# Stacked and exact parts in a linear attention's two kinds of products, with SyncE copies between partitions, and three seams reordered

## What is computed

```python
q, k, v = x @ Wq, x @ Wk, x @ Wv                    # 16 heads of 16
gk = log_sigmoid(x @ Wgk1 @ Wgk2 + bgk2) / 16       # decay of each feature
def step(state, inp):
    qt, kt, vt, gt = inp
    state = state * exp(gt)[..., None] + vt[..., None] * kt[..., None, :]
    return state, einsum('bhvk,bhk->bhv', state, qt)
out = layernorm(outs) * gamma + beta
out = (out * silu(x @ Wg)) @ Wout
x = x + out * silu(mixture_of_adapters(x))          # first layer
x = x + window_attention(x) * silu(ternary_mlp(x))  # second layer, left out here
```

## Time and profile before

| | us |
|---|---|
| median of 3 runs (3458.78 to 3458.85) | 3458.81 |
| the profiled execution | 3460.7 |
| its span in the trace | 3459.0 |
| from chunk 0 of one sequence to that of the next | 212.0 |

### The profile page before, as it was taken

How to read it: one execution, slowest core, us unless ns; L and a number is a source line. 1 busy time by engine, 2 the same in 40 slices (tenths; PEclk the granted TensorE clock), 3 DMA queues, 4 the chain that set the end, 5 groups by cost and what they waited for, 6 DMA issues and landing times.

```text
span 3459.0 us, 88576 instructions
## 1 busy us (share of the span) xinstructions
PE 3342.5 (97%) x34556; PEld 2274.0 (66%) x34556; DVE 2607.4 (75%) x6329; ACT 1863.8 (54%) x4135; POOL 1273.4 (37%) x1393
## 2 busy tenths in 40 slices
PE   6999999999999999999999999999999999999998
PEld 3676666766666666666666666666676666766666
DVE  6777867778677777877778777786777867778777
ACT  3364654646546465463655636456364653646546
POOL 4424244242442524325233342423434244242442
PEclk8999999999999999999999999999999999999999
DMA  4001010010110101011010100101001010010110
GB/s 105 18 22 47 24 38 19 24 44 24 38 23 24 40 24 47 14 38 26 24 50 11 50 18 20 49 12 49 18 23 45 24 38 23 20 44 24 38 23 26
DMA packets 98479, 109.59 MB, mean 32 GB/s; under 512 B 21153, under 2 KB 75025, under 8 KB 98065
## 3 DMA queue, kind: packets, MB, share of 16 engines
q1 hardware_dynamic: 93200, 102.25, 11.3%
q10 hardware_dynamic: 4864, 1.69, 0.2%
HBM read 74.01 MB, written 17.30 MB: 26 GB/s over the span
## 4 chain that ended last, share of the span: by engine, by line
PE 75%; DVE 12%; ACT 5%; issue 5%; POOL 1%; DMA 0%; DVEq 0%; SPq 0%; ACTq 0%; POOLq 0%
PE bank L1549 6%; PE bank L1508 5%; PE bank L1879 5%; PE bank L1647 5%; PE bank L1529 5%; PE bank L1781 5%; PE bank L1897 4%; PE bank L1719 4%; PE bank L1664 3%; PE bank L1619 3%; PE bank L1816 3%; PE bank L1842 3%; PE bank L1604 3%; PE bank L1713 2%; DVE am L1245 2%
## 5 line engine op out<-in xcount | busy, mean ns | idle before, releaser
L867 POOL TENSOR_TENSOR qx<-qx 128x512 f32<-128x512 f32 x256 | 277.3, 1088 | 658.7 <-ACT qx L1113 657.8
L1470 DVE TENSOR_TENSOR sq_lo<-qx,sq_hi 128x512 fp32r<-128x512 f32 x256 | 224.1, 875 | 177.1 <-ACT sq_hi L1092 176.6
L1378 DVE TENSOR_REDUCE row_max<-bank 128x4 f32<-128x384 f32 x512 | 270.8, 550 | 95.4 <-PE bank L1781 95.0
L1245 DVE TENSOR_TENSOR am<-bank,causal 128x512 f32<-128x512 f32 x512 | 328.1, 683 | 11.3 <-PE bank L1619 11.3
L988 ACT ACTIVATE tanh_g<-bank 128x256 f32<-128x256 f32 x128 | 49.3, 385 | 394.9 <-PE bank L1508 394.9
L1508 PE MATMUL bank<-w_vg,xt 128*128 128x512 f32 x512 | 252.3, 615 | 0.0
L1549 PE MATMUL bank<-xt,w_down 128*128 128x512 f32 x512 | 237.2, 596 | 0.0
L1897 PE MATMUL bank<-sq_hi,pj_t 128*128 128x512 f32 x512 | 213.2, 416 | 14.8 <-DVE sq_lo L1470 10.3
L1387 DVE TENSOR_TENSOR am<-bank,row_max 128x384 f32<-128x384 f32 x384 | 212.8, 554 | 9.8
L1113 ACT ACTIVATE qx<-bank,scale_fc 128x512 f32<-128x512 f32 x256 | 177.9, 695 | 70.9 <-PE bank L1884 69.0
L1032 ACT ACTIVATE am<-am 128x384 f32<-128x384 f32 x384 | 202.9, 528 | 8.5 <-DVE am L1387 8.5
(11 more groups left out here) (264 smaller groups left out, 8671.4 us busy)
## 6 DMA issues: line engine op xcount, KB each, us to landing
g_wide<-gate_rows SPq DMA_DIRECT2D x64, 512.0 KB, 6.0
x<-in_L_attn_x SPq DMA_DIRECT2D x128, 128.0 KB, 2.3
qt<-in_L_attn_x SPq DMA_DIRECT2D x128, 128.0 KB, 2.6
out<-x SPq DMA_DIRECT2D x128, 128.0 KB, 1.7
k<-k SPq DMA_DIRECT2D x96, 128.0 KB, 2.4
qt<-in_L_attn_x ACTq DMA_DIRECT2D x8, 128.0 KB, 7.6
x<-in_L_ffn_w_fc SPq DMA_DIRECT2D x1, 1024.0 KB, 5.9
attn<-in_L_ffn_w_proj SPq DMA_DIRECT2D x1, 1024.0 KB, 8.7
```

The lines of the kernel that those rows point to most:

```text
L867: nc.gpsimd.tensor_tensor(sq[:, n % 3, :], relu[:, n % 3, :], relu[:, n % 3, :], ALU.mult)\
L1245: nc.vector.tensor_tensor(am_tiles[:, :, j], bank[3 + j][:].rearrange("p (f e t) -> p f e t", f=2, e=2), causal[:].unsqueeze(1).unsqueeze( ...
L1378: nc.vector.tensor_reduce(row_max[:, j, :], bank[1 + j][:, 0:4 * KW].rearrange("p (h k) -> p h k", k=KW), AX.X, ALU.max, negate=(j == 0)). ...
L1470: nc.vector.tensor_tensor(sq_lo[:, n % 3, :], sq[:, n % 3, :], sq_hi[:, n % 3, :].bitcast(F32), ALU.subtract)\
```

## The change

**Decays' sums.** SP copies halves of the two parts between partitions (`decay_moves`), so that one tile holds, in its 128 rows, high and low part of the chunk's first 64 tokens, another those of the last 64. Each is summed by one product, so a chunk has four products in the place of six. Where they waited for POOL they now wait for the last of SP's copies (`gkd_ok`).

**Score products of chunks 1 to 7.** ACT writes rounded queries and keys (`split_highs`, two copies of 512 columns), DVE the queries' rests (`split_queries`, 512 columns), POOL the keys' rests (`split_keys`, 256 columns), and SP copies 16 rows at a time into the rows that were zero (`split_moves`, 16 DMAs a chunk). PE then makes 32 fp32r products of 128 columns in the place of 16 instructions of 256. POOL's masked queries are left for chunk 0 alone. The two stacked tiles take turns, and SP's copies of a chunk must all have landed before its scores (`split_done[c]`).

**Seams.** An activation of one column (`warm`) makes ACT load its exponentials' table between two adapters' activations of the start; `attention_bias` stands one pair earlier for two steps of the second attention; the normalisations of the next sequence move from MLP steps 6, 7, 8, 9 to 6, 7, 9, 10, and its rstd from steps 4 and 7 to 5 and 8.

```diff
@@ SP
+def split_moves(c):
+    sp.wait_ge(s["spq_ok"], at("spq_ok", c))
+    sp.wait_ge(s["spk_ok"], at("spk_ok", c))
+    tile = stacked[c % 2]
+    for e in range(2):
+        for j in range(4):
+            here = slice(32 * j + DH * e, 32 * j + DH * e + DH)
+            there = slice(32 * j + DH * (1 - e), 32 * j + DH * (1 - e) + DH)
+            sp.dma_start(tile[there, 0, e].bitcast(F32), k_low[here, c % 2]).then_inc(split_done[c], 16)
+            sp.dma_start(tile[there, 1:3, e].bitcast(F32), tile[here, 1:3, e].bitcast(F32)).then_inc(split_done[c], 16)
+def decay_moves(i):
+    two, low, high = slice(2 * i, 2 * i + 2), slice(0, QB), slice(QB, P)
+    sp.wait_ge(s["gkh_ok"], at("gkh_ok", i + 1))
+    sp.dma_start(gk_second[high, two, :].bitcast(F32), gk_first[high, two, :].bitcast(F32))
+      .then_inc(s["gkm_ok"], 16)
+    sp.wait_ge(s["gkl_ok"], at("gkl_ok", i + 1))
+    if i:
+        sp.wait_ge(s["gkd_ok"], at("gkd_ok", 32 * i))
+    sp.dma_start(gk_second[low, two, :].bitcast(F32), gk_low[high, two, :]).then_inc(s["gkd_ok"], 16)
+    sp.wait_ge(s["gkm_ok"], at("gkm_ok", 16 * (i + 1)))
+    sp.dma_start(gk_first[high, two, :].bitcast(F32), gk_low[low, two, :]).then_inc(s["gkd_ok"], 16)
+decay_moves(0)
 for g in range(NG):
+    if g:
+        for i in range(1, NC // 2):
+            decay_moves(i)
+        for c in range(1, 4):
+            split_moves(c)
     sp.wait_ge(s["gx_ok"], at("gx_ok", g + 1))
...
+for c in range(4, NC):
+    split_moves(c)
@@ ACT
+    nc.scalar.activation(warm[:], gdiff[:, 0:1], ACT.Exp)
     experts_relu(3)
...
+def split_highs(c):
+    if c >= 3:
+        act.wait_ge(s["at_ok"], at("at_ok", 4 * c - 4))
+    cols = slice(c * P, (c + 1) * P)
+    nc.scalar.copy(stacked[c % 2][:, 1], qt[:, :, cols].unsqueeze(1).broadcast_to([P, 2, 2, P]))
+    nc.scalar.copy(stacked[c % 2][:, 0], kt[:, :, cols].unsqueeze(1).broadcast_to([P, 2, 2, P]))
+      .then_inc(s["sph_ok"], 1)
+split_highs(1)
 for c in range(NC):
+    if c + 2 < NC:
+        split_highs(c + 2)
@@ DVE
     if c + 1 < NC:
         experts_gate(c)
+    if c == 0:
+        split_queries(1)
+    if c + 2 < NC:
+        split_queries(c + 2)
@@ POOL
-    parity_queries(c + 1)
+    if c == 0:
+        split_keys(1)
     hidden_gated(c + 1)
+    if c + 2 < NC:
+        split_keys(c + 2)
@@ PE, cumulate(c)
-pe.wait_ge(s["gkl_ok"], at("gkl_ok", c // 2 + 1))
+pe.wait_ge(s["gkd_ok"], at("gkd_ok", 32 * (c // 2 + 1)))
...
-    nc.tensor.matmul(out, cumulator[:, i, :], gk_hi[:, c, :], start=True, stop=False)
-    mm = nc.tensor.matmul(out, cumulator[:, i, :], gk_lo[:, c, :], start=False, stop=True)
+nc.tensor.matmul(bank[3][:, 0:D], cumulator[:, 0, :], first, start=True, stop=False)
+nc.tensor.matmul(bank[3][:, 0:D], cumulator[:, 1, :], second, start=False, stop=True)
+nc.tensor.matmul(bank[4][:, 0:D], cumulator[:, 2, :], first, start=True, stop=True)
+mm = nc.tensor.matmul(bank[4][:, D:2 * D], cumulator[:, 2, :], second, start=True, stop=True)
@@ PE, parity_scores(c)
-pe.wait_ge(s["qx_ok"], at("qx_ok", c + 1))
+if c == 0:
+    pe.wait_ge(s["qx_ok"], at("qx_ok", 1))
+else:
+    pe.wait_ge(split_done[c], at("split_done", 16 * 16))
...
+for half in range(2):
+    for e in range(2):
+        for part in range(2):
+            for j in range(4):
+                rows = slice(32 * j, 32 * j + 32)
+                mm = nc.tensor.matmul(bank[3 + j][:, (2 * half + e) * P:(2 * half + e + 1) * P],
+                                      tile[rows, 0, e, half, :], tile[rows, 1 + part, e, half, :],
+                                      start=(part == 0), stop=(part == 1), skip_group_check=True)
@@ DVE, second attention and MLP
+                        if 0 < c < 3:
+                            attention_bias(c - 1)
                         maxima(4 * c + 7)
                         shifted(4 * c + 7)
-                        if c:
+                        if c >= 3:
                             attention_bias(c - 1)
...
-                        if 6 <= n < 10:
+                        if n in normalise_steps:
```

More of the change, by code:

```diff
@@ L113, in build_program @@
     gden = sb("gden", [P, NC])
+    warm = sb("warm", [P, 1])
     g_top = sb("g_top", [P, 2, NC])
@@ L200, in build_program @@
     ft = kt[:, :, 0:512]
+    stacked = tuple(tile[:].rearrange("p b t -> p (b t)").rearrange("p (i e f t) -> p i e f t", i=3, e=2, f=2)
+                    for tile in (sq_hi, sq_lo))
     hidden_t = (qx_flat[:, 8 * P:8 * P + EB // P * 512].rearrange("p (j t) -> p j t", j=EB // P),
@@ L212, in build_program @@
     b_nat = am_flat[:, 3 * D + 3 * P:4 * D + 3 * P]
-    cum_mid, first_half, second_half = (am_flat[:, 3 * D + i * P:3 * D + (i + 1) * P] for i in range(3))
+    cum_first, cum_second, all_ones = (am_flat[:, 3 * D + i * P:3 * D + (i + 1) * P] for i in range(3))
     fc_nat, pj_ter = x, kt
@@ L303, in build_program @@
     low_banks = (2, 0)
+    split_done = [sem(f"split_done{c}") for c in range(NC)]
     x_in = [sem(f"x_in{c}") for c in range(NC)]
@@ L523, in _ @@
                                          pattern=[[1, P]], channel_multiplier=-1))
-            link(nc.gpsimd.tensor_copy(cum_mid[:], causal[:]))
-            link(nc.gpsimd.tensor_scalar(cum_mid[0:QB, :], cum_mid[0:QB, :], -1.0, None, ALU.add))
-            link(nc.gpsimd.memset(first_half[QB:P, :], 0.0))
-            link(nc.gpsimd.memset(second_half[QB:P, :], 1.0))
-            for i, t in enumerate((cum_mid, first_half, second_half)):
+            link(nc.gpsimd.memset(cum_second[:, QB:P], 1.0))
+            for half in range(2):
+                rows = slice(half * QB, (half + 1) * QB)
+                for t, cols, fill in ((cum_first, slice(0, QB), -1.0), (cum_second, slice(QB, P), 0.0)):
+                    link(nc.gpsimd.affine_select(out=t[rows, cols], in_=t[rows, cols], compare_op=ALU.is_ge, fill=fill,
+                                                 base=0, pattern=[[1, QB]], channel_multiplier=-1))
+            for i, t in enumerate((cum_first, cum_second, all_ones)):
                 link(nc.gpsimd.tensor_copy(cumulator[:, i, :], t[:]))
@@ L868, in _ @@
                           .then_inc(s["sq_ok"], 1)
[L869 to L870 removed]
+                        if n in (5, 8):
+                            head_rstd(pool, n // 8)
                 now["copy"] = 0
@@ L1197, in _ @@
                         dve.wait_ge(s["gk_ok"], at("gk_ok", i + 1))
-                        nc.vector.tensor_copy(gk_hi[:, two, :], gk[:, two, :]).then_inc(s["gkh_ok"], 1)
+                        nc.vector.tensor_copy(gk_first[:, two, :], gk[:, two, :]).then_inc(s["gkh_ok"], 1)
                     dve.wait_ge(s["xc_ok"], at("xc_ok", 16 * NC))
@@ L1615, in parity_scores @@
                             pe.wait_ge(s["hr_ok"], at("hr_ok", 4 + c))
-                        for half in range(2):
-                            for j in range(4):
-                                rows = slice(32 * j, 32 * j + 32)
-                                mm = nc.tensor.matmul(bank[3 + j][:, half * 2 * P:(half + 1) * 2 * P],
-                                                      kt[rows, half, c * P:(c + 1) * P], qp[rows, c % 2, half],
-                                                      start=True, stop=True)
-                                if half:
-                                    mm.then_inc(s["at_ok"], 1)
+                        if c == 0:
+                            for half in range(2):
+                                for j in range(4):
+                                    rows = slice(32 * j, 32 * j + 32)
+                                    mm = nc.tensor.matmul(bank[3 + j][:, half * 2 * P:(half + 1) * 2 * P],
+                                                          kt[rows, half, 0:P], qp[rows, half], start=True, stop=True)
+                                    if half:
+                                        mm.then_inc(s["at_ok"], 1)
+                            return
+                        tile = stacked[c % 2]
+                        for half in range(2):
+                            for e in range(2):
+                                for part in range(2):
+                                    for j in range(4):
+                                        rows = slice(32 * j, 32 * j + 32)
+                                        mm = nc.tensor.matmul(bank[3 + j][:, (2 * half + e) * P:(2 * half + e + 1) * P],
+                                                              tile[rows, 0, e, half, :], tile[rows, 1 + part, e, half, :],
+                                                              start=(part == 0), stop=(part == 1), skip_group_check=True)
+                                        if half and e and part:
+                                            mm.then_inc(s["at_ok"], 1)
                     def pair_turn(p):
```

67 lines of the change are left out of this document (39 added, 28 removed).

## The result

| | before | after |
|---|---|---|
| median, us | 3458.8 | 3825.46 (3822.61 to 3832.15) |
| ratio, 95% interval | | 1.1064 (1.1045 to 1.1083) |
| span of the profiled execution, us | 3459.0 | 3819.9 |

The kernel is slower by 366.7 us, 22.9 us in each of the 16 sequences. Forecast were 10.0, and 3825 lies above the range that ended at 3710. The side was right, the size was not.

What follows compares the result with a forecast made beforehand. PE was taken as the bound, with SP's added issues deciding. Chunk 1's delay 9.4 + clock 2.1 - decays' sums 0.82 - scores 0.1 - seams 0.6 = 10.0 us a sequence, x 16 = 160: 3619 us, range 3540 to 3710.

Steps and rivals of the forecast that it cites:

- signs: Expected on PE: about 8 us idle ahead of chunk 1's scores, none ahead of chunks 2 to 7; wrong if before each.
- step 5: SP's sixteen copies for chunk 1: eight at 0.43 us, eight at 0.60, 8.25 in all; scores 9.4 us later.
- Chunks 2 to 7: SP's 8.25 us of issues a chunk keep up with chunks of 10.6, later 9.3 to 9.6 us; no wait.
- steps 2 to 4: Chunk 0: gate rows 1.86 us later, then nine later decays' copies on SP; chunk 1's copies start at 1571.5.
- The rival that SP is the bound of every chunk: At 0.75 us an issue, chunk 1 comes 13.5 us later and the next six take 12 each: 3855 us, chance 9%.
- Step 1: First decays' copies on SP, chunk 0: issued until 1555.95, nothing lost for the decays' sums, 0.4 us of slack.
- Step 2: Chunk 0: gate rows 1.86 us later, so experts_up waits from 1565.16 until 1566.4; the table load's 1.28 us ends there.
- The clock behind the stall: PE's lower clock after its wait ahead of chunk 1 costs another 2.1 us, bounds 1 and 2.4.
- Score products: The 32 products on PE run at the weights' pace, 0.11 us a round, 1.05 us in all; gain 0.03 a chunk.
- Both rivals on the products' pace: Score products at the columns' pace, 3579 us, chance 8%; or at 0.22 us a round, 3692 us, chance 8%.
- Decays' sums: Two products fewer a chunk on PE: 0.72 us gained in chunks 1 to 3, 0.1 in all of chunks 4 to 7.
- Seams: Earlier attention_bias and moved normalisation free PE from waits of 0.84 us a sequence together, of which 0.6 was taken.

Runs made afterwards that it cites:

- eight: The changed kernel with only eight of the sixteen copies for each chunk's score products (e = 0 alone): 3616.3 us, ratio 1.0454.
- no_copies: The changed kernel without the sixteen copies a chunk; PE waits for the splits themselves, and the 32 products stay: 3505.8 us, ratio 1.0132.
- decays: The changed kernel with masked queries and 16 score instructions as before, keeping the changed decays' sums and the seams: 3493.0 us, ratio 1.0097.
- the seams: The kernel before with the early exponentials' table, the earlier attention_bias and the moved normalisations alone: 3426.4 us, ratio 0.9908.
- decays_gate: decays with the first gate rows issued between the first and the second copy of decay_moves(0): 3445.9 us, ratio 0.9958.

## Why the prediction was wrong, point by point

**The bound now, and the shape of the change.** Right: PE bound the chunks, SP's issues decided, and the longest stall came ahead of chunk 1, put down to the DMA that was named. Its idle time, 8.89 us, is near the "about 8" of the signs by luck: the scores came 13.5 us later where 9.4 were forecast, but PE too arrived late, held up in chunk 0. Waits ahead of chunks 4 to 7 were one of the prediction's own signs of being wrong, and they came.

**The failed step: the price of an issue** (step 5, and with it "Chunks 2 to 7"). Eight of the sixteen copies were put at 0.43 us, the price of loads of `x` with 128 partitions, and the chunk at 8.25 us. They cost 0.63 and 0.66, and one in 25 is a long one: a chunk has 10.9 us in the mean, 11.4 in the sequence shown. The trace of before had this price for copies within SBUF: 64 times a copy of keys follows another directly, and the median distance of the starts is 0.656, the mean 0.677. The prediction divided the 1.87 us of three copies by three and used the result for half of its copies alone. Two things follow.

- *Chunk 1.* Counted from the end of the loads of `x` its scores stood at 19.0 us before and stand at 32.5 after, 13.5 later where 9.4 were forecast. The copies started 1.28 us later than steps 2 to 4 said, from the first issue to the last were 10.82 in the place of 7.65, and from there to the scores 2.06 in the place of 2.4: 1.28 + 3.17 - 0.34 = 4.1, the difference.
- *Chunks 2 to 7.* The prediction had no wait in them. SP has 10.2 to 11.8 us of issues for chunks of 9.3 to 10.85 us, so it falls behind: +8.2 us a sequence, the largest single miss, 131 of the 206 us between 3619 and 3825. In `eight` 0.4 of the 8.2 is left. For chunk 5 the prediction's cycle (copies can start 7.4 us behind the scores two chunks earlier) also left out POOL's order: they started 12.8 us behind.

The rival that SP is the bound of every chunk said this, with 3855 us. Its price of 0.75 us an issue was too high, so that it came within 30 us of the measured time is in part luck. Its point of decision, 0.66 us, was worked out for a chunk of 10.6 us, and the mean distance is 0.680; for the later chunks of 9.3 to 9.63 us the same division gives 0.58 to 0.60, which even the median distance of 0.646 exceeds. I gave it 9% on the ground that no row of ten or more issues was that slow, but the trace of before had no row of ten small copies at all: an absence was read as evidence.

**Steps 1 to 3.** Step 1 held, and the gate rows went out 2.97 us behind the loads (2.81 forecast). Step 2 had 1 to 1.3 us of wait for `experts_up`; it was 3.0. Counted from the end of the loads the eight products stood at 12.02 before and at 14.15 after, 2.1 later where 1.24 were forecast: from the gate rows to `g_wide` were 2.0 us in the place of 1.5, and from there to POOL's product 7.9 in the place of 7.6. The other 0.9 is PE, which `warm` let arrive earlier; the prediction named this and left it out of the size of the wait. Behind the wait came a loss by the clock that it didn't have: 3.78 us for eight products that took 1.89, at a granted clock of 0.50.

**The clock behind the stall.** Right: chunk 1 took 2.3 us more (2.1 forecast). The granted clock was 0.75 and 0.81 in the stretches of chunk 0 and chunk 1, between the levels of 2.4 and 1.2 GHz, and 1.00 in the next:

```profile
1719.50:1744.10 24.60, 12.78 (x82) 8.80 (x81) 7.51 (x17) 6.33 (x15) 8.81 (x11) 0.75 0.40 95
1744.10:1757.00 12.90, 12.82 (x103) 8.97 (x103) 6.13 (x13) 4.72 (x11) 0.74 (x1) 0.81 0.15 38
1757.00:1767.70 10.70, 10.70 (x104) 7.64 (x103) 9.02 (x22) 4.72 (x11) 5.31 (x7) 1.00 0.17 39
```

**Score products.** Right: from 1757.03 the 32 products took 1.04 us until the next line started (1.05 forecast), so the weights' pace of the earlier trace rows held. Rounds lie 0.11 us apart. The Trainium skill (TensorE: Matmul & The Clock Gate, LDWEIGHTS) has a load last P / 1.2 ns for P columns, 107 for 128, whatever the rows. This trace agrees in the pace, 0.11 us from round to round with 32 rows here as with 128 in the earlier trace rows, though its rows show each load for 0.18 to 0.19 us. Both rivals on the products' pace fall. The whole part is worth 0.04 us a chunk and costs 0.8 a sequence elsewhere, copies apart (`no_copies`).

**Decays' sums.** Too high: 0.82 a sequence forecast, 0.14 measured (`decays` against the seams, the three distances from chunk 1 to 4). The four products lie 0.12 us apart and end 0.24 sooner, but in chunk 1 the product behind them waits for DVE's mask just as long. PE in `decays_gate`:

```profile
1573.10 0.71 PE L1748 MATMUL bank<-qt,state_mid 128*128 128x128 f32 x4 [0.23 <-DVE am L1275]
```

The cover that I had assumed for chunks 4 to 7 alone is there before them too.

**Seams.** Too low: 0.6 forecast, 2.07 measured. The 0.75 us of the table's load were written off against step 2's wait, and the rest was cut from 0.84 for risks that did not come.
